# A hybrid attention and expert layer: the first sixteen row maxima read from tiles filled on the chip, one direct transfer per shift, and expert up-weights split in pieces

## The chip, the cores and the metric

One core of a Trainium2 chip runs the whole layer in one launch. The metric is the device time in microseconds of one execution; three executions were timed.

## The reference, cut to what matters

The input is 2 sequences of 1024 tokens with 128 channels. Four blocks follow, each with a residual and a layer norm: differential attention, a mixture of 64 experts (8 chosen for each token, plus a shared one), an attention over heads, and the same experts again. The change touches the start of the first block and what it shares the engines with:

```python
q, k, v = split(layernorm(x) @ w_qkv.T)          # 16 heads, 2 sub-heads of 4 channels each
s = einsum('bnhd,bmhd->bhnm', qi, ki) * scale    # 32 sub-heads, each 1024 x 1024, per sequence
p = softmax(s)                                   # the maximum over the keys is taken off
a = einsum('bhnm,bmhe->bhne', p, v)              # o = a1 - lam * a2, rms norm, w_proj
h = silu(einsum('td,edf->etf', xf, W_up))        # experts, read in high and low parts
y = einsum('etf,efd->etd', h, W_down)
```

## The kernel before, in words

Every engine has its own instruction stream, written out by hand, and they meet by semaphores. TensorE does matmuls, VectorE the row maxima, ScalarE the exponentials, GpSimd small arithmetic, SyncE nearly all transfers.

**Beginning.** The tokens are four chunks of 512 columns. For each chunk VectorE takes statistics and normalizes (`stats`, `norm`), GpSimd computes the inverse roots (`root_of`), TensorE transposes (L1239) and multiplies by the query and key weights (`queries_and_keys`, L1249), and each result is split in three bf16 parts that sum to the float32 value: ScalarE writes the high part (L814), VectorE the rest (L1024), ScalarE the middle part (L818), VectorE the low part (L1029). The values (`va`, L1255) come after all chunks.

**Stacks.** The query and key parts are laid out in DRAM, in `q_stack` and `k_stack`: 16 groups of 4 sub-heads ("strips" of 32 rows), each holding six slots of 4 rows and then rows for the shift, which `fill_shift_rows` presets. `write_parts` issues twelve transfers of 256 KB for each sequence (L479). `load_max` reads a group back into `QA` and `KA`; `load_strips` reads it into `QB` and `KB`.

**Max pass.** For each group 32 items, each a 128 x 1024 tile of scores, made by two matmuls (L1296) into two PSUM banks, of which VectorE takes the negated row maximum (`NEGMAX`, L1067). The items have two places in PSUM, banks 0-1 and 2-3. There are 512 items.

**Main loop.** A quad is two items of the max pass, four score tiles (L1333) with their exponentials (L860), and the weighted values of the quad before (L1360). There are 16 x 16 quads. The max pass leads by `LEAD` quads: quads -12 to -1 only take maxima, and the last 12 only have scores, together with side work for the experts (`SIDE`): a chain of transposes, affinities and top-k that ends in a gate tile and the `GATE` transfers. `PE` runs a quad in the order: score, item, score, weighted values, score, item, score, weighted values.

**Shifts.** After 16 items GpSimd splits their 16 columns of maxima in three bf16 parts (`shift_parts`), TensorE transposes them (L1305, at quads where `shift_at` says so, five items before the scores that need them), VectorE copies the tile out (`SHT`, L1080), SyncE writes it to `shift_d` in DRAM (L530) and reads it back into rows of `QB` in four transfers (L535). So the matmul of the scores subtracts the maximum by itself. The scores of a half group wait for it (`sh_r`). In PE's order the next item stands behind those scores.

**Expert weights.** ScalarE issues the transfers of `RAWD` (L799) and `RAWU` (four, L805), copies the high part of each (`WDH` L841, `WUH` L847), and GpSimd subtracts for the low part (L627), all before the first exponential. ScalarE also evacuates the output tiles every eight quads.

## Time and profile before

| | us |
|---|---|
| median of three executions | 1083.62 |
| lowest and highest | 1078.84, 1085.8 |
| the profiled execution, device time | 1082.55 |
| its span, first to last instruction | 1080.8 |
| VectorE busy | 958.7 (89%) |
| TensorE busy | 1001.8 (93%) |
| ScalarE busy | 890.6 (82%) |

The profile is of one execution. Its page gives the busy time of each engine, a strip of 40 slices, a chain of what ended last, and the costliest groups of instructions. The trace answers closer questions: the order of instructions in a stretch, the busy time of each engine in a stretch with the clock granted to TensorE, what an engine waited for, and how long transfers took from issue to landing. "L1067" is a line of the kernel.

### The profile page before, as it was taken

How to read it: one execution, taken by the hardware profiler on the slowest of the kernel's cores; microseconds unless marked ns; L12 is line 12 of the kernel's file. 1: busy time of each engine (PE TensorE's matmuls, PEld its weight loads, DVE VectorE, ACT ScalarE, POOL GpSimd, SP SyncE). 2: the span in 40 equal slices, each digit the busy share in tenths (PEclk: the TensorE clock that was granted, in tenths of full speed). 3: DMA queues.
4: the chain of work that ended last, by engine and by line, in shares of the span. 5: the costliest groups of instructions: out<-in, count | busy, mean ns of one | idle time of the engine just before them, and what ended most of it. 6: DMA issues, size and time to landing. Idle time of an engine off the chain costs nothing.

```text
span 1080.8 us, 21671 instructions
## 1 busy us (share of the span) xinstructions
PE 1001.8 (93%) x8016; PEld 517.0 (48%) x8016; DVE 958.7 (89%) x1187; ACT 890.6 (82%) x1466; POOL 482.7 (45%) x892
## 2 busy tenths in 40 slices
PE   6389999999999999999999999999999999999998
PEld 3012222232222222222222236888777778787876
DVE  7799999999999999999999956989876978797665
ACT  4279999999999999999999987878865787688765
POOL 3363555455445645564555657443412331333331
PEclk9569999999999999999999999999999999999999
DMA  8911110111011011101110007585766566757773
GB/s 276 306 34 51 52 51 4 51 51 32 23 52 51 17 37 52 51 3 51 52 52 3 22 3 171 151 195 146 173 179 156 137 161 174 194 153 188 197 187 91
DMA packets 80474, 108.91 MB, mean 101 GB/s; under 512 B 23537, under 2 KB 33521, under 8 KB 80369
## 3 DMA queue, kind: packets, MB, share of 16 engines
q1 hardware_dynamic: 66336, 100.98, 35.0%
q10 hardware_dynamic: 14032, 6.55, 2.4%
q8 instruction: 64, 1.05, 0.4%
q14 instruction: 42, 0.34, 0.1%
HBM read 95.57 MB, written 11.93 MB: 99 GB/s over the span
## 4 chain that ended last, share of the span: by engine, by line
DVE 51%; PE 33%; ACT 5%; DMA 4%; issue 4%; SPq 1%; POOL 0%; ACTq 0%; DVEq 0%; POOLq 0%
DVE NEGMAX L1067 46%; PE PS L1458 9%; PE PS L1460 8%; PE PS L1459 8%; PE PS L1360 3%; ACT PR L860 2%; PE PS L1333 1%; DVE HF L1108 1%; DVE HL L1116 1%; DMA shift_d<-SHT 1%; DMA GATE<-gate_d 1%; ACT PS L957 1%; ACT HH L950 1%; PE PS L1239 1%; DVE XC L1014 1%
## 5 line engine op out<-in xcount | busy, mean ns | idle before, releaser
L1067 DVE TENSOR_REDUCE NEGMAX<-PS 128x1 f32<-128x1024 f32 x512 | 584.9, 1211 | 10.2 <-PE PS L1296 9.9
L860 ACT ACTIVATE PR<-PS 128x512 f32<-128x512 f32 x1024 | 539.0, 600 | 36.7 <-PE PS L1333 24.7
L1360 PE MATMUL PS<-PR,VG 128*32 128x256 f32 (+1 forms) x3840 | 321.9, 407 | 17.3 <-ACT PR L860 2.0
L1333 PE MATMUL PS<-QB,KB 32*128 32x512 bf16 x1024 | 260.1, 387 | 3.6 <-DMA QB<-shift_d 2.1
L1296 PE MATMUL PS<-KA,QA 32*128 32x512 bf16 x1024 | 204.6, 397 | 30.7 <-DVE NEGMAX L1067 22.5
L1108 DVE TENSOR_TENSOR HF<-PS,GATE 128x1024 f32<-128x1024 f32 x128 | 156.3, 1222 | 65.0 <-ACT PS L957 55.2
L957 ACT ACTIVATE PS<-PS 128x1024 f32<-128x1024 f32 x128 | 129.2, 1009 | 75.5 <-PE PS L1460 74.4
L1333 PEld LDWEIGHTS PS<-QB,KB 32*128 32x128 bf16 x1024 | 75.2, 91 | 240.5 <-ACT PR L860 138.7
L950 ACT ACTIVATE HH<-HF 128x1024 fp32r<-128x1024 f32 (+1 forms) x136 | 139.8, 1029 | 24.2 <-DVE HF L1108 23.1
L769 POOL TENSOR_TENSOR HL<-HF,HH 128x1024 fp32r<-128x1024 f32 (+1 forms) x31 | 66.8, 2154 | 165.5 <-ACT HH L950 165.5
L1360 PEld LDWEIGHTS PS<-PR,VG 128*32 128x32 f32 x3840 | 76.4, 108 | 130.7 <-issue 65.0
L1116 DVE TENSOR_TENSOR HL<-HF,HH 128x1024 fp32r<-128x1024 f32 (+1 forms) x105 | 131.9, 1257 | 7.6 <-ACT HH L950 7.5
L1458 PE MATMUL PS<-XH,WUH 128*128 128x512 f32 x256 | 107.8, 421 | 0.0
L1458 PE MATMUL PS<-HH,WDH 128*128 128x512 f32 x256 | 102.5, 400 | 2.5 <-ACT YS L967 2.5
L1460 PE MATMUL PS<-HH,WDL 128*128 128x512 f32 x256 | 101.5, 396 | 0.0
L1459 PE MATMUL PS<-XL,WUH 128*128 128x512 f32 x256 | 101.4, 396 | 0.0
L1460 PE MATMUL PS<-XH,WUL 128*128 128x512 f32 x256 | 101.1, 395 | 0.0
L1459 PE MATMUL PS<-HL,WDH 128*128 128x512 f32 x256 | 100.8, 394 | 0.0
L675 POOL TENSOR_TENSOR ORC<-OSB,MINUS 128x16 f32<-128x16 f32 x32 | 93.2, 2911 | 3.3 <-DVE OSB L1093 0.9
L641 POOL TENSOR_TENSOR SHP<-NEGMAX,ZERO 128x16 bf16<-128x16 f32 x32 | 7.0, 218 | 167.2 <-DVE NEGMAX L1067 167.1
L1296 PEld LDWEIGHTS PS<-KA,QA 32*128 32x128 bf16 x1024 | 48.3, 91 | 58.5 <-DVE NEGMAX L1067 45.1
L1458 PEld LDWEIGHTS PS<-HH,WDH 128*128 128x128 f32 x256 | 48.4, 189 | 15.4 <-ACT YS L967 4.6
(186 smaller groups left out, 971.6 us busy)
## 6 DMA issues: line engine op xcount, KB each, us to landing
GATE<-gate_d SPq DMA_DIRECT2D x256, 256.0 KB, 4.2
QA<-q_stack SPq DMA_DIRECT2D x64, 128.0 KB, 2.6
QB<-q_stack SPq DMA_DIRECT2D x16, 256.0 KB, 3.0
KB<-k_stack SPq DMA_DIRECT2D x16, 256.0 KB, 3.0
KA<-k_stack SPq DMA_DIRECT2D x60, 64.0 KB, 2.4
q_stack<-PARTS SPq DMA_DIRECT2D x12, 256.0 KB, 4.4
k_stack<-PARTS SPq DMA_DIRECT2D x12, 256.0 KB, 4.2
RAWU<-in_L_ffn_W_up_dram ACTq DMA_DIRECT2D x4, 512.0 KB, 11.6
```

Source lines behind the costliest of these rows:

```text
L860: nc.scalar.activation(PR[:, s % PRING, r, :], PS[:, SCORE_BANK[n], :], ACT.Exp, scale=SCALE_A).then_inc(p_ready, 1)
L950: nc.scalar.activation(HH[:, k, 0:u, :], HF[:, f, 0:u, :], ACT.Copy).then_inc(hh_ok, 1)
L957: nc.scalar.activation(PS[:, z:z + 2, :], PS[:, z:z + 2, :], ACT.Silu).then_inc(silu_ok, 1)
L1067: nc.vector.tensor_reduce(NEGMAX[:, hs % 2, col:col + 1], PS[:, e:e + 2, :].rearrange("p b n -> p (b n)"), axis=AX_X, op=ALU.max, negate=T ...
L1108: nc.vector.tensor_tensor(HF[:, k, :, :], PS[:, z:z + 2, :], GATE[:, h % GSLOTS, :, :], op=ALU.mult).then_inc(hf_ok, 1)
L1116: nc.vector.tensor_tensor(HL[:, k, 0:u, :], HF[:, f, 0:u, :], HH[:, k, 0:u, :].bitcast(F32), op=ALU.subtract).then_inc(hl_ok, 1)
L1296: last = mm(PS[:, e + h, :], QA[lo:lo + STRIP, u, r // 2, nt * P:(nt + 1) * P], KA[lo:lo + STRIP, u, r // 2, :], start=True, stop=True)
L1333: mm(PS[:, SCORE_BANK[n], :], KB[strip, u, mt * P:(mt + 1) * P], QB[strip, u, half * BANK:(half + 1) * BANK], start=True, stop=True).then_ ...
L1360: last = mm(PS[STRIP * r:STRIP * (r + 1), 7, cols], VG[:, u, mt, r // 2, :], PR[:, s % PRING, r, cols], start=mt == 0, stop=mt == TB - 1 a ...
L1458: mm(dst, ah, bh, start=first, stop=False)
L1459: mm(dst, ah, bl, start=False, stop=False)
L1460: return mm(dst, al, bh, start=False, stop=last)
```

## The change

- SyncE loads two chunks of the input ahead of the weights. VectorE presets `QB` and `KB`; after the parts of the first two chunks exist, SyncE copies the rows of the first group from `PARTS` to `QB` and `KB` in twelve transfers of 16 rows of 2 KB. The first 16 items read these; items 16 to 31 of the first group read `QA` and `KA` as before, which are now loaded wholly by SyncE.
- The slots of the stacks are interleaved (row, slot), and the parts of one kind go out in one transfer, six for each sequence instead of twelve.
- The low parts of chunks 0, 2 and 3 move from VectorE to GpSimd. The orders of all engines in the beginning are rewritten; TensorE runs ten matmuls whose result is not used.
- The first 16 items have three places in PSUM (banks 0-1, 2-3, 6-7).
- `LEAD` is 11; the shift tile comes one quad later (three items before its scores) and goes to `QB` by one transfer, with no DRAM in between.
- `RAWU` is loaded in 16 transfers and split in 8 pieces through the main loop: ScalarE copies 512 columns at quads 28, 44, ... 140, GpSimd subtracts. Its addition of the projection bias to `X` moves into the loop as well.

```diff
-STACK_WRITES = 16 * 2 * (len(Q_SLOTS) + 1)
+SLOTS = STRIP // HD_A
+SHIFT_SLOT = SLOTS - 1
+STACK_WRITES = 16 * 2 * 4
+FIRST_LOADS = 16 * 2 * len(Q_SLOTS)
...
-LEAD = 12
+LEAD = 11
...
-    return (g + 3) // TB if (g + 3) % TB == 0 and 0 <= (g + 3) // TB < 2 * NG else None
+    return (g + 2) // TB if (g + 2) % TB == 0 and 0 <= (g + 2) // TB < 2 * NG else None
...
+def max_slots():
+    start = []
+    for it in range(len(ITEM)):
+        start.append((0, 2, 6)[it % 3] if it < 2 * TB else 2 * ((it + 1) % 2))
+    before = [max((m for m in range(max(0, it - 3), it) if start[m] == start[it]), default=None) for it in range(len(ITEM))]
+    return start, before
+MAX_SLOT, MAX_BEFORE = max_slots()
...
-A_ITEM = ring_order(["wT"] + [("xT", c) for c in range(NCH)] + [("va", c) for c in range(NCH)] + ["centT"])
+A_ITEM = ring_order(["wT", ("xT", 0), ("xT", 1), ("xT", 2), ("va", 0), ("va", 1), "centT", ("xT", 3), ("va", 2), ("va", 3)])
+A_LATE = A_ITEM["va", 2]
...
+def up_piece(s):
+    k = (s - 28) // QPG
+    return k if s >= 28 and (s - 28) % QPG == 0 and k < UP_PIECES else None
...
@@ sync @@
+            load_x(0)
+            load_x(1)
+            sp.dma_start(WQKV[:], w_qkv.rearrange("(j p) c -> p j c", p=P)).then_inc(ld_w, 16)
+            sp.dma_start(WPRJ[:], w_proj).then_inc(ld_w, 16)
+            load_x(2)
+            load_x(3)
+            sp.wait_ge(const_ok, 2)
...
+                    step = places[1] - places[0] if len(places) > 1 else 1
+                    rows = stack[b * GPB:(b + 1) * GPB].rearrange("g r d c n -> (g r d) c n")[:, places[0]:places[-1] + 1:step, :]
+                    sp.dma_start(rows, src.unsqueeze(1).to_broadcast([P, len(places), SEQ])).then_inc(st_w[b], 16)
...
+            def first_rows(part, j):
+                tile, slots = ((QB, Q_SLOTS), (KB, K_SLOTS))[j]
+                for c in [c for c, a in enumerate(slots) if a == part]:
+                    sp.dma_start(tile[c:P:SLOTS, 0, :], PARTS[0:R * HD_A, part, j, 0:SEQ]).then_inc(first_ld, 16)
...
             fill_shift_rows(0)
+            sp.dma_start(CENT[:], cent).then_inc(ld_b, 16)
+            for j, w in enumerate((w_q, w_k, w_v, w_o)):
+                sp.dma_start(WB[:, j, :], w).then_inc(ld_b, 16)
+            sp.wait_ge(first_set, 2)
+            for part, made in enumerate((qk_hi, qk_mid)):
+                for j in range(2):
+                    sp.wait_ge(made, 2 * NCH // BATCH - 1 + j)
+                    first_rows(part, j)
+            for j in range(2):
+                sp.wait_ge(qk_lo_pool, j + 1)
+                sp.wait_ge(qk_lo, j + 1)
+                first_rows(2, j)
+            for part in range(3):
+                write_parts(0, part)
...
-            load_max(0, 0, False)
+            load_max(0, 0)
+            fill_shift_rows(1)
+            for part, (made, n) in enumerate(((qk_hi, 2 * NCH), (qk_mid, 2 * NCH), (qk_lo_pool, 6))):
+                sp.wait_ge(made, n)
+                write_parts(1, part)
+            load_max(1, 1)
+            sp.wait_ge(const_ok, 3)
...
-                sp.dma_start(shift_d[half].rearrange("a r (t n) -> (a r t) n", n=P), SHT[:, half, :]).then_inc(sh_w, 16)
-                sp.wait_ge(sh_w, 48 * s + 16 * (half + 2))
-                for r in range(R):
-                    lo = STRIP * r + SHIFT_ROW
-                    sp.dma_start(QB[lo:lo + 3, u, half * BANK:(half + 1) * BANK], shift_d[half, :, r, :]).then_inc(sh_r, 16)
+                sp.dma_start(QB[SHIFT_SLOT:P:SLOTS, u, half * BANK:(half + 1) * BANK], SHT[:, half, :]).then_inc(sh_r, 16)
...
                     shift_rows(s, half)
+                    if s < UP_PIECES:
+                        load_up(2 * s + half)
...
@@ gpsimd @@
+            def low_part(c):
+                cols = slice(c * BANK, (c + 1) * BANK)
+                for j in range(2):
+                    n = D_ITEM["qk", j, c]
+                    pool.wait_ge(qk_mid, n + 1)
+                    nc.gpsimd.tensor_tensor(PARTS[:, 2, j, cols], R1[:, n % 4, :], PARTS[:, 1, j, cols], op=ALU.subtract).then_inc(qk_lo_pool, 1)
             for c in range(NCH):
                 root_of(("a", c))
+            for c in (0, 2, 3):
+                low_part(c)
...
+            low_weights(0, WDL[:], RAWD[:], WDH[:])
+            pool.wait_ge(ld_mix, 16 * 9)
+            for j in range(2):
+                link(nc.gpsimd.tensor_tensor(lam_p[:, j, :], LAM[:, 2 * j, :], LAM[:, 2 * j + 1, :], op=ALU.mult))
...
+            shift_parts(0)
             values(0, 0)
             values(1, 1)
-            link(nc.gpsimd.memset(ZERO[:], 0.0))
-            shift_parts(0)
-            low_weights(1, WUL, RAWU, WUH)
             for n, (dst, src, hi) in enumerate(((WSUL, RAWSU, WSUH), (WSDL, RAWSD, WSDH))):
-                low_weights(n + 2, dst, src, hi)
+                low_weights(n + 1, dst[:], src[:], hi[:])
...
+                if hs == 3:
+                    pool.wait_ge(ln_xn, NCH)
+                    nc.gpsimd.tensor_tensor(X[:], X[:], BPROJ[:].unsqueeze(1).to_broadcast([P, NT, DIM]), op=ALU.add).then_inc(xb_ok, 1)
+                if hs >= 6 and hs % 2 == 0 and hs // 2 - 3 < UP_PIECES:
+                    low_up(hs // 2 - 3)
...
@@ scalar @@
+            transposed(0)
+            high_part(0, 0)
+            transposed(1)
+            high_part(1, 0)
+            middle_part(0, 0)
+            high_part(0, 1)
+            high_part(1, 1)
+            middle_part(1, 0)
+            middle_part(0, 1)
+            middle_part(1, 1)
+            transposed(2)
+            values(0)
+            values(1)
+            centroids()
+            high_part(0, 2)
+            transposed(3)
+            high_part(1, 2)
+            middle_part(0, 2)
+            middle_part(1, 2)
+            high_part(0, 3)
+            high_part(1, 3)
+            middle_part(0, 3)
+            middle_part(1, 3)
+            values(2)
+            values(3)
             act.wait_ge(ld_down, 16)
             nc.scalar.activation(WDH[:], RAWD[:], ACT.Copy).then_inc(w_hi, 1)
-            for part in range(4):
-                load_up(part)
-            act.wait_ge(ld_exp, 32)
-            act.wait_ge(ld_up, 16 * 4)
-            for dst, src in ((WUH, RAWU), (WSUH, RAWSU), (WSDH, RAWSD)):
-                nc.scalar.activation(dst[:], src[:], ACT.Copy).then_inc(w_hi, 1)
             act.wait_ge(lam_in, 1)
             nc.scalar.activation(lam_e[:], lam_s[:], ACT.Exp).then_inc(lam_exp, 1)
+            act.wait_ge(ld_exp, 32)
+            for dst, src in ((WSUH, RAWSU), (WSDH, RAWSD)):
+                nc.scalar.activation(dst[:], src[:], ACT.Copy).then_inc(w_hi, 1)
...
+            def high_up(k):
+                cols = slice(k * BANK, (k + 1) * BANK)
+                act.wait_ge(ld_up, 16 * UP_PARTS // UP_PIECES * (k + 1))
+                nc.scalar.activation(WUH[:, cols], RAWU[:, cols], ACT.Copy).then_inc(w_hi, 1)
...
+                if up_piece(s) is not None:
+                    high_up(up_piece(s))
...
@@ vector @@
+            nc.vector.memset(QB[:, 0, :], 0.0).then_inc(first_set, 1)
+            nc.vector.memset(KB[:, 0, :], 1.0).then_inc(first_set, 1)
             for c in range(NCH):
                 dve.wait_ge(ld_x[c], 16)
                 stats(("a", c))
-                if c:
+                if 1 <= c <= 2:
                     norm(("a", c - 1))
-            norm(("a", NCH - 1))
-            for c in range(NCH):
-                rest_and_low(c)
-            dve.wait_ge(ld_mix, 16 * 9)
-            for j in range(2):
-                link(nc.vector.tensor_tensor(lam_p[:, j, :], LAM[:, 2 * j, :], LAM[:, 2 * j + 1, :], op=ALU.mult))
-            nc.vector.tensor_reduce(lam_s[:], lam_p[:], axis=AX_X, op=ALU.add).then_inc(lam_in, 1)
-            link(nc.vector.tensor_scalar(SUBW[:], SUBW[:], 1.0 - LAMBDA_INIT, None, ALU.mult))
+            rest(0, 0)
+            norm(("a", 2))
+            rest(1, 0)
+            rest(0, 1)
+            rest(1, 1)
+            low_part(0, 1)
+            low_part(1, 1)
+            norm(("a", 3))
...
+            for c in range(2, NCH):
+                rest(0, c)
+                rest(1, c)
...
@@ tensor @@
+            def warm(times):
+                for _ in range(times):
+                    mm(PS[:, 7, :], identb[:], ONES[:, 0:BANK], start=True, stop=True)
             pe.wait_ge(ident_ok, 1)
+            pe.wait_ge(identb_ok, 1)
+            pe.wait_ge(const_ok, 2)
+            warm(4)
...
+            warm(6)
+            transposed(0)
+            copied(0)
+            query_or_key(0, 0)
+            transposed(1)
+            query_or_key(1, 0)
+            copied(1)
+            query_or_key(0, 1)
+            query_or_key(1, 1)
+            transposed(2)
+            values(0)
+            values(1)
+            centroids()
+            copied(2)
+            query_or_key(0, 2)
+            query_or_key(1, 2)
+            transposed(3)
+            copied(3)
+            query_or_key(0, 3)
+            query_or_key(1, 3)
+            values(2)
+            pe.wait_ge(first_ld, FIRST_LOADS)
...
-                    e = 2 * (it % 2)
-                    if it >= 2:
-                        pe.wait_ge(m_free, it - 1)
+                    e = MAX_SLOT[it]
+                    if MAX_BEFORE[it] is not None:
+                        pe.wait_ge(m_free, MAX_BEFORE[it] + 1)
+                    elif e == 6:
+                        pe.wait_ge(qk_r1, len(D_ITEM))
...
+                    if hs == 0:
+                        strip = slice(STRIP * r, STRIP * (r + 1))
+                        for h in range(2):
+                            last = mm(PS[:, e + h, :], QB[strip, 0, nt * P:(nt + 1) * P],
+                                      KB[strip, 0, h * BANK:(h + 1) * BANK], start=True, stop=True)
+                        last.then_inc(m_full, 1)
+                        if it == 1:
+                            values(3)
+                        continue
+                    if a == 0 or hs == 1:
```

## Rows read from the trace of the kernel before

**Rows 1.** The page: the costliest group, busy time, mean of one, idle before, releaser
```profile
L1067 DVE TENSOR_REDUCE NEGMAX<-PS 128x1 f32<-128x1024 f32 x512 | 584.9, 1211 | 10.2 <-PE PS L1296 9.9
```
**Rows 2.** Stretches: length, PE, PEld, DVE, ACT, POOL busy, granted clock, DMA share, GB/s
```profile
20.00:30.00 10.00, 6.79 (x40) 4.68 (x38) 8.04 (x18) 7.91 (x17) 0.00 (x0) 1.00 0.86 319
40.00:50.00 10.00, 5.28 (x18) 0.82 (x17) 10.00 (x10) 0.00 (x0) 4.49 (x1) 0.50 1.14 359
60.00:70.00 10.00, 8.75 (x44) 1.53 (x44) 9.11 (x9) 6.70 (x14) 8.94 (x2) 0.50 0.01 2
100.00:200.00 100.00, 94.88 (x1029) 29.60 (x1025) 99.85 (x93) 94.75 (x187) 51.86 (x124) 1.00 0.15 42
625.60:654.00 28.40, 25.85 (x265) 9.56 (x258) 12.28 (x41) 24.77 (x49) 19.80 (x41) 1.00 0.04 12
```
**Rows 3.** What VectorE waited for from 80 to 610 us: total, times, longest
```profile
DVE NEGMAX L1067 <- PE PS L1296: 1.3, 5, 0.3
```
**Rows 4.** The chain of waits, first 110 us: start, length, what
```profile
26.35 2.87 DMA k_stack<-PARTS
36.30 21.57 DVE NEGMAX L1067 x19
```
**Rows 5.** Timeline of the beginning: start, length, engine, line, what
```profile
12.07 3.62 PE L1249 MATMUL PS<-XT,WT 128*128 128x512 f32 x4
12.42 1.11 DVE L1014 TENSOR_SCALAR XC<-X,ln_mv,ln_inv 128x128 f32<-128x128 f32 x4
16.34 2.23 PE L1249 MATMUL PS<-XT,WT 128*128 128x512 f32 x4
16.53 1.23 ACT L818 ACTIVATE PARTS<-SQ 128x512 bf16<-128x512 f32 x2 [0.20 <-DVE SQ L1024]
18.41 0.60 PE L1239 MATMUL PS<-ident,XC 128*128 128x128 f32 x4
26.11 1.29 DVE L1029 TENSOR_TENSOR PARTS<-SQ,PARTS 128x512 bf16<-128x512 f32 x2 [0.17 <-ACT PARTS L818]
28.11 0.38 DVE L1047 TENSOR_REDUCE T<-ident 128x8 f32<-128x128 f32 x1
28.85 0.23 DVE L1049 COPY BLK<-H 128x128 f32<-128x128 f32 x1
31.99 3.62 ACT L841 ACTIVATE WDH<-RAWD 128x4096 fp32r<-128x4096 f32 x1 [3.15 <-issue]
35.68 8.81 POOL L627 TENSOR_TENSOR WDL<-RAWD,WDH 128x4096 fp32r<-128x4096 f32 x1 [20.94 <-ACT WDH L841]
```
**Rows 6.** VectorE's low parts of the experts: duration in ns min/median/max
```profile
L1116 DVE TENSOR_TENSOR HL<-HF,HH x105: 684/1215/2977, 660.9 to 1072.4; 128x1024 fp32r<-128x1024 f32 x104, 128x512 fp32r<-128x512 f32 x1
```
**Rows 7.** Timeline of SyncE, then ScalarE's issues of RAWU, ns min/median/max
```profile
26.35 0.61 SPq L479 DMA_DIRECT2D k_stack<-PARTS  x1
59.78 1.20 SPq L535 DMA_DIRECT2D QB<-shift_d  x4
652.09 10.28 SPq L573 DMA_DIRECT2D GATE<-gate_d  x10
L805 ACTq DMA_DIRECT2D RAWU<-in_L_ffn_W_up_dram x4: 572/3502/4652, 32.0 to 40.0; - x4
```
**Rows 8.** Transfers of the first 60 us: count, KB each, median us to landing
```profile
q_stack<-PARTS SPq DMA_DIRECT2D x12, 256.0 KB, 4.4
BPROJ<-in_L_attn_a_b_proj_dram SPq DMA_DIRECT2D x1, 64.0 KB, 9.0
```
**Rows 9.** Timeline of a shift copy, and landing of the DRAM write behind each
```profile
77.68 0.21 DVE L1080 COPY SHT<-PS 48x128 bf16<-48x128 bf16 x1
DMA to landing us min/median/max: 1.3/1.4/2.9
```
**Rows 10.** The page: gate transfers, median to landing
```profile
GATE<-gate_d SPq DMA_DIRECT2D x256, 256.0 KB, 4.2
```
**Rows 11.** Timeline of VectorE: its first gated product after the attention
```profile
658.60 2.35 DVE L1108 TENSOR_TENSOR HF<-PS,GATE 128x1024 f32<-128x1024 f32 x2
```

More of the change, by code:

```diff
@@ L116, in score_tiles @@
                 tiles["out", output_at(g)] = len(tiles)
-        if shift_at(g) is not None:
-            tiles["shift", shift_at(g)] = len(tiles)
+            if p == 1 and shift_at(g) is not None:
+                tiles["shift", shift_at(g)] = len(tiles)
     return tiles
@@ L364, in hybrid_layer @@
         OTS = sb("OTS", [P, 2, BANK], where=attn)
-        SHP = sb("SHP", [P, 2, 3 * SHIFTS], BF16, where=attn)
-        SHT = sb("SHT", [3 * SHIFTS, 2, P], BF16, where=attn)
+        SHP = sb("SHP", [P, 2, R, 4, SHIFTS // R], BF16, where=attn)
+        SHT = sb("SHT", [4 * SHIFTS, 2, P], BF16, where=attn)
         ZERO = sb("ZERO", [P, SHIFTS], where=attn)
@@ L646, in shift_parts @@
                 pool.wait_ge(sh_split, (4 * hs + 3))
-                nc.gpsimd.tensor_tensor(SHP[:, u, 2 * w:3 * w], SHR[:], SHP[:, u, w:2 * w], op=ALU.subtract).then_inc(sh_split, 1)
+                nc.gpsimd.tensor_tensor(SHP[:, u, :, 2, :], rest, SHP[:, u, :, 1, :], op=ALU.subtract).then_inc(sh_split, 1)
                 pool.wait_ge(sh_split, (4 * hs + 4))
-            low_weights(0, WDL, RAWD, WDH)
-            for b in range(BATCH):
-                pool.wait_ge(st_w[b], STACK_WRITES)
+            link(nc.gpsimd.memset(ZERO[:], 0.0))
@@ L773, in _ @@
                 side(where)
-                if where == NQ - 11:
+                if where == NQ - 10:
                     heads_norm(2 * NG - 3)
@@ L1233, in ring @@
                     pe.wait_ge(free, n - 3)
-                put((0 if items is A_ITEM else 4) + n % 4).then_inc(full, 1)
+                put(a_bank(n) if items is A_ITEM else 4 + n % 4).then_inc(full, 1)
             def transposes(tiles):
@@ L1377, in quad @@
                     weighted_values(s - 1, 0)
+                if shift_at(s) is not None:
+                    shift_tile(shift_at(s))
                 if scored:
```

225 lines of the change are left out of this document (103 added, 122 removed).

## The prediction

> **What bounds the kernel now.** I read the page first. One line, the row maximum on VectorE, is busy 584.9 us of the 1080.8 us span and sits idle only 10.2 us before its instructions [rows 1]. The stretches of time say where it rules: from 100 to 200 us VectorE is busy 99.85 of 100, TensorE 94.88, ScalarE 94.75 [rows 2], and over 530 us of the loop the maxima waited 1.3 us in all [rows 3]. So the attention lasts as long as its 512 maxima, and nothing that another engine saves there counts, while 5% of slack is all that either neighbour has. The chain of waits then shows where the maxima begin: the write of the key stack and the read back precede 36.30 us, after which 19 maxima run in 21.57 us, 1.13 each [rows 4]. VectorE had finished all parts at 27.4 (26.11 + 1.29 [rows 5]), those of the first sequence earlier. The gap from 27.4 to 36.3 is the trip through DRAM. That trip is what the change takes out.
>
> **The first maximum.** With the rows copied on the chip, the limit becomes the order of work on VectorE. Its old work ended at 27.4 (26.11 + 1.29). Of its 16 rests and low parts, at 1.29 a pair, six go to GpSimd: minus 6 x 0.645 = 3.9. The three constants, 28.11 to 29.08, now stand ahead of the maxima: plus 1.0 [rows 5]. That gives 24.5. ScalarE, with 0.62 for each middle part, and TensorE, with 1.12 for a product at the full clock (2.23 for two items against 3.62 at half clock, 12.07 and 16.34 [rows 5]), come out at the same time when I lay the three orders side by side; the ten unused matmuls keep TensorE from being late, by bringing the full clock to the first chunk. One thing more: the low parts on GpSimd and on VectorE both read two tiles of SBUF at once. In the experts, where both engines do exactly that, VectorE's instruction takes 1215 ns as a rule but up to 2977 [rows 6], so one can stand behind the other. I add 0.5, for one GpSimd low part of about 1.1 (8.81 for 4096 columns [rows 5]) met half way: **25.0 us**.
>
> The Trainium skill (SBUF — State Buffer, "SBUF: two separate sides") says the pair of ports that the two share is locked for a whole instruction and the loser blocks fully. The trace's 2977 ns agrees. By that rule alone up to three meetings of 1.1 us would be possible here, so a start 3 us later.
>
> The twelve row transfers do not decide. SyncE issues four small ones in 1.20 [rows 7], so twelve in 3.6, most of them before the last low part at 18.5; landing takes 4.4 in the busy early stretch [rows 8], so they land by 23.2. The bound above: a small transfer issued into that crowd landed after 9.0 [rows 8], which gives 27.5 for the start. The bound below is 24.0, if the port meeting is nothing and the full clock comes earlier. Gain: 36.3 - 25.0 = **11.3** (8.8 to 12.3).
>
> **The third place in PSUM.** Between 40 and 50 us VectorE was busy 10.00 of 10 with two places, at half clock [rows 2]. There is nothing to win: 0. It only covers the value matmuls put behind item 1. In both versions these 16 items take 18.1 us.
>
> **SyncE until the first shift.** Now SyncE must have come past 41 issues between the last small rows (18.5) and the shift: 6 stack writes, 9 constants, 8 loads, 2 fills, 6 writes, 8 loads, 2 shared weights. At 0.65 each (0.61 and a gap [rows 7]) this is 26.7: 45.2. The shift copy comes 21.6 after the first maximum, at 46.6. So it fits, by 1.4. Data: 8.5 MB at 319 to 359 GB/s [rows 2] take 24 to 27 us from 18.5, 43 to 45.5. It fits too, barely. But the merged writes are three times as large, and four large transfers in a crowded queue took 572 to 4652 ns to issue [rows 7]. If each of the twelve costs 1.0 rather than 0.65, SyncE arrives at 49.4, and the first scores with it; behind it also ScalarE, whose first exponential now waits for the shared weights, the last two of the 41. Cost 0 to 4.5; I take **0.5**, nearer the 0.61 row, since these are pieces of 2 KB as there and the 2 MB of `RAWU` that crowded the queue from 32 us on are gone. The group for items 16 to 31 is wanted at 43 and is issued by about 34: covered by 18 us of maxima. GpSimd: `WDL` takes 8.81 after `WDH` of 3.62 [rows 5], started at about 26, done at 38.6 against 43.1, when the first shift is split.
>
> **The direct shift.** The copy lasts 0.21, the write to DRAM landed 1.4 after its issue (1.3 to 2.9) [rows 9]. For one hop in place of two I take the same: 1.65 after the copy's start. The deadline shrinks by two items of 1.13: three maxima (3.4) and the copy's 0.1, less one score and one item on TensorE, 0.7, leaves 2.8. So it is in time as a rule, and 0.3 late at the slowest. Loss **0.2** (0 to 9, if all 32 are at the slow end). Queued behind a late shift are the scores and, in TensorE's order, the next item, so lateness goes straight to VectorE.
>
> **Weights in pieces.** `WUH` and the `RAWU` transfers lay beside the maxima and cost nothing on the path. Eight copies of 512 columns, 0.62 each by a middle part [rows 5], now interrupt the exponentials: 5.0 us of ScalarE where it has 5% slack, 0.96 for eight quads. They stand three quads after the output copies, when that slack is partly used. Bounds 0 and 5.0; I take **1.0**. GpSimd is half busy [rows 2] and its bias and low pieces stay hidden; without that cover each low piece would cost 1.1.
>
> **One quad less of lead.** The total is lead-in, 512 maxima, and a tail of `LEAD` quads. The tail was 28.4 us for 12, ScalarE 24.77 of it [rows 2]: 2.06 a quad. But the gate chain begins relative to the last maximum as before: the first gate transfers, issued from 652.09 at about 0.6 each [rows 7], land 4.2 later [rows 10], at 656.9, and the first gated product ran at 658.60 [rows 11]. So only **1.7** is free (0 to 2.1); next late is the gate.
>
> **Half clock at the first scores.** TensorE ran at 0.50 from 40 to 70 us, and VectorE lost 0.89 of 10 in the last ten [rows 2]. With little to do in the lead it will be at half clock again: 0. If it stays at 1.00, a gain of 0.9.
>
> **Sum.** 11.3 + 1.7 - 0.5 - 0.2 - 1.0 = 11.3 off 1082.55, the profiled execution (span 1080.8 and 1.75 around it), which is 1.07 below the median of the three: 1071.3, and I say **1071.5**.
>
> **Rivals.** (1) *SyncE late*: twelve merged writes above 1.0 each; first scores and first exponential late by 4. For it: issue times up to 4652 ns in a crowd. Against: 0.61 for the same rows, in the full stretch before 27 us. Result 1075. (2) *ScalarE becomes the bound* at the eight pieces and pays them whole: 1075.5. For it: 94.75 busy; against: TensorE's two places ahead of VectorE absorb about 0.7 (an item of 1.13 less its two matmuls of some 0.4). (3) *The shift late every time*, the slower outcome: a half group's scores wait on a transfer onto sixteen-row-spread partitions that lands like the gate transfers, 4.2 after issue [rows 10]. From 2.8 on each microsecond is paid 32 times: (0.25 + 4.2 - 2.8) x 32 = 53, less 11.5: 1124. Against it: 16 KB, not 256, and 1.4 in the nearest row. It decides from a landing of 3.3 on, where it has eaten the gain. (4) *The start does not move as said*, because rows, ports or orders hold it to 27.5 or later: 1074. (5) *All well*: start at 24.0, full clock kept, no late wait: 1068.
>
> **Chances.** Forecast 0.47, (1) 0.19, (2) 0.10, (3) 0.04, (4) 0.08, (5) 0.12. About 1% is what a measurement of this kernel can tell from no change; that is 10.8 us, below 1072.8. The forecast gives it in four of five cases, (5) always: 0.51. Slower by over 1% only in (3): 0.04. Within: 0.45. For the range I go down to 1065 (case 5 and executions that spread by 0.4%) and up to 1080, (1) and (2) together with the late start.
>
> **What would show it.** Right: first maximum at 24 to 26 us; `SHT` about 21.6 later; no wait of the maxima above 0.3 through the loop; SyncE at the shift before VectorE's copy; the last maximum about 11 us earlier; about 1 us of waits near quads 28 + 16k. Wrong: waits of the scores on the transfer to `QB` in many periods (3), a first exponential that starts late behind shared weights (1), or a first maximum after 27.

## The result, and the profile after

The changed kernel takes 1085.96 us (median of 19 executions, 1081.33 to 1094.18), the kernel before 1081.13 (19 executions beside them, 1078.59 to 1085.8). The ratio is 1.0046, 95% interval 1.0032 to 1.0059: slower by 4.8 us. The forecast was 1071.5, within 1065 to 1080; the time lies above the range. The profiled execution after has a span of 1087.0 us, that of before 1080.8. Labels in this part: "L1157" is now the maximum, "L1430" the products of the items from `QA` and `KA`, "L1420" those from `QB` and `KB`, "L1469" the scores, "L1170" the copy of the shift tile. In the experiments the same lines have slightly other numbers. A ratio and its interval compare a kernel with the executions of the kernel before that stood beside it; it is not exactly the quotient of the two medians.

The page's line of the maximum, busy time, mean of one, idle before it and its releaser:

```profile
L1157 DVE TENSOR_REDUCE NEGMAX<-PS 128x1 f32<-128x1024 f32 x512 | 585.2, 1211 | 15.7 <-PE PS L1430 15.1
```

Against [rows 1] the work is the same, 585 us. The idle time is 15.7 instead of 10.2, and 15.1 of it waits for a product. The timeline of VectorE from 25 to 70 us shows where:

```profile
25.62 21.59 DVE L1157 TENSOR_REDUCE NEGMAX<-PS 128x1 f32<-128x1024 f32 x19
47.13 0.21 DVE L1170 COPY SHT<-PS 64x128 bf16<-64x128 bf16 x1
47.26 3.47 DVE L1157 TENSOR_REDUCE NEGMAX<-PS 128x1 f32<-128x1024 f32 x3
60.28 4.62 DVE L1157 TENSOR_REDUCE NEGMAX<-PS 128x1 f32<-128x1024 f32 x4 [9.55 <-PE PS L1430]
65.95 1.22 DVE L1157 TENSOR_REDUCE NEGMAX<-PS 128x1 f32<-128x1024 f32 x1 [1.06 <-PE PS L1430]
```

The first maximum runs at 25.62 instead of 36.30 [rows 4]: 10.7 us won. Nineteen maxima and the copy follow as before. Then three more, and VectorE stands still for 9.55 us. The product that it waits for stands in TensorE's order behind scores, and the scores wait for the shift, as the list of TensorE's waits shows (total, times, longest):

```profile
PE PS L1469 <- DMA QB<-SHT: 10.4, 1, 10.4
```

The timeline of SyncE says why the shift was late. It lists issues (start, length, destination and source); I leave out the lines inside runs of equal ones:

```profile
15.86 1.96 SPq L514 DMA_DIRECT2D QB<-PARTS  x3
22.98 0.53 SPq L514 DMA_DIRECT2D KB<-PARTS  x1
23.56 0.58 SPq L508 DMA_DIRECT2D q_stack<-PARTS  x1
...
28.60 1.64 SPq L508 DMA_DIRECT2D k_stack<-PARTS  x1
30.28 1.83 SPq L532 DMA_DIRECT2D LAM<-n_L_attn_a_lambda_q_dram  x1
...
36.20 0.49 SPq L548 DMA_DIRECT2D QA<-q_stack  x1
...
41.21 0.59 SPq L500 DMA_DIRECT2D q_stack<-ZEROS  x1
...
42.35 0.90 SPq L508 DMA_DIRECT2D q_stack<-PARTS  x1
...
48.74 1.24 SPq L508 DMA_DIRECT2D k_stack<-PARTS  x1
50.02 1.25 SPq L548 DMA_DIRECT2D QA<-q_stack  x1
...
57.16 0.47 SPq L563 DMA_DIRECT2D RAWSD<-in_L_ffn_Ws_down_dram  x1
57.73 0.59 SPq L578 DMA_DIRECT2D QB<-SHT  x1
```

The shift tile was ready at 47.3 and SyncE issued its transfer at 57.73. It was never idle in between; it worked off its list. ScalarE came no earlier, since the shared weights are the two issues before the shift. Its timeline:

```profile
59.21 0.31 ACT L924 ACTIVATE WSUH<-RAWSU 128x128 fp32r<-128x128 f32 x1 [18.20 <-DMA RAWSD<-in_L_ffn_Ws_down_dram]
60.26 2.06 ACT L941 ACTIVATE PR<-PS 128x512 f32<-128x512 f32 x4 [0.54 <-PE PS L1469]
```

Were these issues slow because of the data, or by themselves? Stretches of four microseconds tell (length, busy PE, PEld, DVE, ACT, POOL, granted clock, DMA share, GB/s):

```profile
28.00:32.00 4.00, 2.38 (x8) 0.46 (x8) 4.00 (x4) 2.81 (x1) 2.40 (x6) 0.90 1.03 377
32.00:36.00 4.00, 3.59 (x9) 0.43 (x8) 4.00 (x5) 0.00 (x0) 4.00 (x1) 0.50 0.33 103
36.00:40.00 4.00, 3.70 (x8) 0.45 (x8) 4.00 (x4) 0.00 (x0) 3.93 (x2) 0.50 0.50 124
44.00:48.00 4.00, 2.54 (x9) 0.46 (x7) 4.00 (x5) 0.00 (x0) 1.37 (x6) 0.50 1.03 376
100.00:200.00 100.00, 93.12 (x1001) 29.58 (x993) 97.21 (x90) 93.10 (x184) 57.74 (x126) 1.00 0.18 48
```

Both. During the large writes (24 to 30, 42 to 50 us) the DMA engines are full, share 1.03 and 377 GB/s, and the issues run little ahead of the data: one sequence's six writes are 3.1 MB, 8.3 us at that rate, and took 6.7 and 7.7 to issue. During the constants and the eight loads (32 to 40) they are half empty, share 0.33 and 0.50: there the issues themselves are the limit. The last row, compared with [rows 2], shows that VectorE is busy 97.21 us from 100 to 200 us, no longer 99.85; in the four stretches of 100 us behind it, it is busy 99.26 to 99.97. What VectorE waited for, first from 58 to 620 us, then from 80 to 615 (total, times, longest):

```profile
DVE NEGMAX L1157 <- PE PS L1430: 15.1, 15, 9.6
DVE NEGMAX L1157 <- PE PS L1430: 3.9, 11, 0.9
```

The second answers to 1.3 in [rows 3]. The last maximum ends at 627.99 (614.16 in before plus 11.48 is 625.64). So after a start that is 10.7 earlier, the end of the maxima is 2.35 **later**: 12.4 us more of waits (15.1 against 1.3 and 1.4 more before 80 us) and 0.6 of small pauses.

The shift's landing, from issue, min/median/max, answers to [rows 9]; the page's gate transfers to [rows 10]:

```profile
DMA to landing us min/median/max: 1.7/1.8/3.7
GATE<-gate_d SPq DMA_DIRECT2D x256, 256.0 KB, 4.1
```

And the tail, on VectorE's timeline, answers to [rows 11]:

```profile
659.56 1.22 DVE L1198 TENSOR_TENSOR HF<-PS,GATE 128x1024 f32<-128x1024 f32 x1 [0.74 <-DMA GATE<-gate_d]
661.73 1.23 DVE L1198 TENSOR_TENSOR HF<-PS,GATE 128x1024 f32<-128x1024 f32 x1 [0.94 <-DMA GATE<-gate_d]
```

SyncE issues the first gate transfer at 654.54, 26.55 us after the last maximum; before it was 652.09, 26.45 after. The products now wait for the gate. The first sum of the experts (ScalarE's first copy into `YS`) runs at 716.88 (713.67 before), 3.2 later.

### The profile page after: what moved, and what is told of

The parts are those of the page before. It is cut to its first block, busy times and chain, and to the rows that moved or that the text cites. A ratio compares the mean times of both kernels' runs of the same rounds, so it can differ in the third digit from the quotient of the medians.

```text
span 1087.0 us, 21613 instructions
## 1 busy us (share of the span) xinstructions
PE 1009.2 (93%) x8026; PEld 521.4 (48%) x8026; DVE 957.0 (88%) x1179; ACT 889.2 (82%) x1473; POOL 492.1 (45%) x911
## 4 chain that ended last, share of the span: by engine, by line
PE 37%; DVE 36%; ACT 11%; DMA 6%; issue 5%; SPq 4%; POOL 0%; DVEq 0%; ACTq 0%; POOLq 0%
DVE NEGMAX L1157 30%; PE PS L1594 7%; ACT PR L941 7%; PE PS L1496 7%; PE PS L1596 7%; PE PS L1595 7%; PE PS L1469 4%; DMA GATE<-gate_d 3%; DVE HF L1198 2%; SPq L508 1%; DVE HL L1206 1%; DMA RT<-mixed_d 1%; PE PS L1478 1%; DMA mixed_d<-VP 1%; PE PS L1329 1%
## 5 line engine op out<-in xcount | busy, mean ns | idle before, releaser
L1157 DVE TENSOR_REDUCE NEGMAX<-PS 128x1 f32<-128x1024 f32 x512 | 585.2, 1211 | 15.7 <-PE PS L1430 15.1
L1469 PE MATMUL PS<-QB,KB 32*128 32x512 bf16 x1024 | 262.8, 387 | 15.0 <-DMA QB<-SHT 10.4
L1430 PE MATMUL PS<-KA,QA 32*128 32x512 bf16 x992 | 195.0, 390 | 14.9 <-DVE NEGMAX L1157 12.1
L1469 PEld LDWEIGHTS PS<-QB,KB 32*128 32x128 bf16 x1024 | 78.4, 91 | 239.0 <-ACT PR L941 117.9
L1430 PEld LDWEIGHTS PS<-KA,QA 32*128 32x128 bf16 x992 | 46.8, 91 | 34.9 <-DVE NEGMAX L1157 25.6
```

Of the source, the lines that this page charges most:

```text
L1157: nc.vector.tensor_reduce(NEGMAX[:, hs % 2, col:col + 1], PS[:, e:e + 2, :].rearrange("p b n -> p (b n)"), axis=AX_X, op=ALU.max, negate=T ...
L1430: last = mm(PS[:, e + h, :], QA[lo:lo + STRIP, u, r // 2, nt * P:(nt + 1) * P], KA[lo:lo + STRIP, u, r // 2, :], start=True, stop=True)
L1469: mm(PS[:, SCORE_BANK[n], :], KB[strip, u, mt * P:(mt + 1) * P], QB[strip, u, half * BANK:(half + 1) * BANK], start=True, stop=True).then_ ...
```

## The experiments

The theories, by the names that the expectations use: **T1**, SyncE's list decides: the shift is late because of the issues ahead of it. **T2**, the data decide: the DMA engines had too much to move in the first 55 us, in whatever order or queue. **T3**, a quad less of lead gives nothing, since the gate chain starts relative to the last maximum. A plain count, 0.65 for each issue taken off the list, stood beside them, and later a theory on the notice of the shift.

**e1: the nine constants ahead of the first rows.** A move inside SyncE's list (the two comments stand for nine lines each):

```diff
             for j, w in enumerate((w_q, w_k, w_v, w_o)):
                 sp.dma_start(WB[:, j, :], w).then_inc(ld_b, 16)
+            # the nine transfers into LAM, BPROJ, SUBW, BO, EBIAS
             sp.wait_ge(first_set, 2)
...
-            # the same nine, after write_parts(0, part)
```

> The changed kernel with one edit: SyncE issues the nine constants (LAM, BPROJ, SUBW, BO, EBIAS) in the gap that its queue has before the first row copies, at about 10 to 15 us, instead of between the stack writes and the loads. Theory T1 (the 9.6 us stall of the maxima at the first scores is SyncE's issue order: the shift transfer was issued at 57.7 us, 10.6 after the shift copy): the 5.9 us of constants leave the queue, but the load of the first group then waits for the last stack write to land, at about 34.9 where it now starts at 36.2, so SyncE gains only about 1.3 and the stall falls from 9.6 to about 8.3. Theory T2 (the 16 DMA engines are the limit, not the issuing): the stall stays at 9.6. A plain count of issues, as in my prediction, says 9.6 - 5.9 = 3.7. First maximum stays at 25.6, at most 0.5 later. Time: 1084.5 by T1, 1086 by T2, 1080 by the plain count.

Measured: 1086.01 us (1081.41 to 1096.59, 10 executions), ratio 1.0043 [1.0016, 1.0070]. VectorE's timeline:

```profile
47.00 0.21 DVE L1170 COPY SHT<-PS 64x128 bf16<-64x128 bf16 x1
58.97 3.49 DVE L1157 TENSOR_REDUCE NEGMAX<-PS 128x1 f32<-128x1024 f32 x3 [8.38 <-PE PS L1430]
```

Taking 5.9 us of issues out moved the shift by 1.3 only (57.73 to 56.4). SyncE's timeline shows what took their place:

```profile
28.50 1.25 SPq L508 DMA_DIRECT2D k_stack<-PARTS  x1
34.88 0.49 SPq L548 DMA_DIRECT2D QA<-q_stack  x1
```

From 29.75 to 34.88 SyncE issues nothing. It waits until the six writes have landed, because the loads behind them read what they wrote. In the changed kernel the constants filled just this wait. So the plain count fails and T1 holds only with that wait in the list: the late shift is made of issues *and* of a landing. The stall fell to 8.38, where T1 said 8.3 and T2 9.6; the time, 1086.0, is the one that T2 gave, and can't tell the two apart.

**e2: the list split over two queues** (from e1). SyncE goes straight on to the second sequence's writes; ScalarE issues the sixteen loads and the shared weights.

```diff
@@ sync @@
-            sp.wait_ge(st_w[0], STACK_WRITES)
-            load_max(0, 0)
...
-            load_max(1, 1)
-            sp.wait_ge(const_ok, 3)
-            sp.dma_start(RAWSU[:, 0:F], ws_up).then_inc(ld_exp, 16)
-            sp.dma_start(RAWSD[0:F, :], ws_down).then_inc(ld_exp, 16)
@@ scalar, behind WDH @@
+            act.wait_ge(const_ok, 3)
+            act.dma_start(RAWSU[:, 0:F], ws_up).then_inc(ld_exp, 16)
+            act.dma_start(RAWSD[0:F, :], ws_down).then_inc(ld_exp, 16)
+            act.wait_ge(st_w[0], STACK_WRITES)
+            load_first(0, 0)
+            load_first(1, 1)
```

> As e1, and the eight loads for the first group, the eight for the second and the two shared expert weights are issued by ScalarE, which is idle from 31 to 59 us; SyncE goes straight from the first sequence's stack writes to the second's. The bytes and their kind stay the same. T1 (issue order): SyncE is free at about 40 us, the shift transfer is issued within 0.3 us of the shift copy at 47.1, the stall falls from 9.6 to under 1, the time falls by about 9, to 1077, and beats the kernel before by 4. T2 (DMA engines saturated): the stall stays above 5, since the same 8.5 MB have to move, and the time stays above 1082.

Measured: 1082.31 us (1077.35 to 1085.56, 10), ratio 1.0000 [0.9978, 1.0022]. VectorE's timeline:

```profile
26.39 18.19 DVE L1168 TENSOR_REDUCE NEGMAX<-PS 128x1 f32<-128x1024 f32 x16
49.61 3.49 DVE L1168 TENSOR_REDUCE NEGMAX<-PS 128x1 f32<-128x1024 f32 x3 [5.04 <-PE PS L1441]
53.02 0.21 DVE L1181 COPY SHT<-PS 64x128 bf16<-64x128 bf16 x1
```

SyncE issues the shift at 53.30, 0.3 after the copy: it is no longer late. But now the 17th item waits 5.04 us, for the loads into `QA` and `KA`. They cannot start before the first writes have landed, and they stand on ScalarE's queue beside SyncE's second writes:

```profile
36.16 0.53 ACTq L918 DMA_DIRECT2D QA<-q_stack  x1
36.73 1.30 ACTq L920 DMA_DIRECT2D KA<-k_stack  x1
...
42.52 1.55 ACTq L920 DMA_DIRECT2D KA<-k_stack  x1
```

and the stretch has no free DMA time:

```profile
36.00:40.00 4.00, 3.69 (x8) 0.38 (x6) 4.00 (x5) 0.00 (x0) 4.00 (x1) 0.50 1.03 371
40.00:44.00 4.00, 2.06 (x5) 0.25 (x4) 4.00 (x5) 0.00 (x0) 1.55 (x6) 0.50 1.04 388
```

The stall and the time are what T2 gave (above 5, above 1082). So T1 holds for the shift, and T2 for what comes next: a second queue lets the loads and the writes share the same engines, and the loads, 0.60 each in the changed kernel, take 1.3 to 1.6. The Trainium skill (Trainium Kernel Development and Optimization, "Key Constraints") says that queues issued from several engines share the 16 DMA engines, and that issuing from more than one saves issue time only. The trace agrees: 1.03 to 1.04 from 28 to 44 us, and half of the stall stays.

**e3: twelve quads of lead, five items of notice** (from e2):

```diff
-LEAD = 11
+LEAD = 12
...
-    return (g + 2) // TB if (g + 2) % TB == 0 and 0 <= (g + 2) // TB < 2 * NG else None
+    return (g + 3) // TB if (g + 3) % TB == 0 and 0 <= (g + 3) // TB < 2 * NG else None
...
-    NQ - 11: [("heads_T", 0)], ...
+    NQ - 12: [("heads_T", 0)], ...
```

> As e2, with LEAD = 12 and the shift tile five items before its scores, as in the kernel before. Theory T3 (the lead gave nothing: after the last maximum the chain to the first gate transfer took 26.5 us in both traces, and the first gated products wait for the gate): same time as e2 within 1 us, the first four gated products at the same distance from the last maximum. Rival (my prediction: a quad less of lead is worth 1.7): e3 slower than e2 by 1.7. Second rival (three items of notice for the shift are too few): e3 faster than e2, by the 2 to 3 us that the maxima lose between 70 and 628 us beside the kernel before.

Measured: 1079.32 us (1077.8 to 1083.92, 10), ratio 0.9993 [0.9973, 1.0012], the interval overlapping that of e2. From the last maximum to the first expert sum it is 89.3 us, e2 has 89.4. In these two profiles a quad more costs nothing at the end, which is T3; and the loop's waits are 1.6 instead of 2.7.

**e4: two places in PSUM** for all items:

```diff
-        start.append((0, 2, 6)[it % 3] if it < 2 * TB else 2 * ((it + 1) % 2))
+        start.append(2 * ((it + 1) % 2))
```

> The changed kernel with one edit: the first 16 maxima have two places in PSUM (as all others) instead of three. My prediction's step says the third place is worth nothing: 1086 within 1 us, VectorE without a gap in the first 16 maxima except up to 0.3 us at item 2, behind the value matmuls. Rival (the third place hides the value matmuls of 0.9 to 1.8 us behind item 1): one gap of 1 us or more there, but it is given back, since the stall at the first scores ends at a time that SyncE sets: same time, stall shorter by the gap.

Measured: 1084.81 us (1082.89 to 1094.03, 10), ratio 1.0044 [1.0017, 1.0071], as the changed kernel. This profile holds an accident that is worth more than the edit. TensorE's and then VectorE's timeline:

```profile
19.42 0.27 PE L1381 MATMUL PS<-ident,CENT 64*128 64x64 f32 x1 [2.84 <-DMA WB<-in_L_attn_b_Wo_dram]
```

```profile
29.20 22.02 DVE L1157 TENSOR_REDUCE NEGMAX<-PS 128x1 f32<-128x1024 f32 x19 [0.16 <-PE PS L1420]
59.65 4.62 DVE L1157 TENSOR_REDUCE NEGMAX<-PS 128x1 f32<-128x1024 f32 x4 [4.91 <-PE PS L1430]
```

In this execution TensorE waited 2.84 us for a weight, and the first maximum ran 3.6 us later than in the changed kernel. The stall was shorter by 4.6, and the maxima resumed at 59.65 against 60.28. SyncE issued the shift at 57.10 as against 57.73. In all three profiles the maxima resume the same time after that issue: 2.55 in the changed kernel, 2.55 here, 2.56 in e1 (56.41 and 58.97). **Where the maxima begin has no effect as long as SyncE's list ends at 57.** The first nineteen maxima took 22.02 instead of 21.59: 0.4 us, in one profile each, is the most that the third place is worth.

**e5: the whole first group from the tiles on the chip** (from e1). Items 16 to 31 read `QB` and `KB` too. So the first group's eight loads go, and the wait for the landing of the first writes moves behind the second ones, where it is over:

```diff
-            sp.wait_ge(st_w[0], STACK_WRITES)
-            load_max(0, 0)
...
+            sp.wait_ge(st_w[0], STACK_WRITES)
             load_max(1, 1)
...
-                    if hs == 0:
+                    if ga == 0:
...
```

> As e1 (constants early on SyncE), and all 32 items of the first group read QB and KB, so its eight loads into QA and KA, and SyncE's wait for the first stacks to land ahead of them, are gone. ScalarE issues nothing new. T1 (order and number of SyncE's issues set the stall): SyncE passes 8 issues and a wait of about 5 us less than in e1, reaches the shift within 1 us of its copy at 47.1, and neither the wait of e2 at item 16 (5.0 us, for loads that crawled behind 4 MB of stack writes) nor the 8.4 us wait at the first scores remains: waits of the maxima under 4 us in all, last maximum at about 618 to 619, time 1077 (5 below the kernel before). Rival T2 (the DMA engines are the limit): the shift transfer or the second group's loads crawl behind the second sequence's writes; at least 4 us of waits remain between 40 and 65 us and the time is that of e2 or worse, 1081 or more.

Measured: 1080.58 us (1074.39 to 1083.45, 10), ratio 0.9995 [0.9974, 1.0015]. SyncE's timeline has the shift nine microseconds earlier:

```profile
48.06 0.59 SPq L577 DMA_DIRECT2D QB<-SHT  x1
```

and VectorE's has no stall above 1.61:

```profile
50.94 4.71 DVE L1156 TENSOR_REDUCE NEGMAX<-PS 128x1 f32<-128x1024 f32 x4 [0.31 <-PE PS L1419]
57.25 10.49 DVE L1156 TENSOR_REDUCE NEGMAX<-PS 128x1 f32<-128x1024 f32 x9 [1.61 <-PE PS L1419]
602.31 14.88 DVE L1156 TENSOR_REDUCE NEGMAX<-PS 128x1 f32<-128x1024 f32 x13
```

The last maximum ends at 617.19, 10.8 us before that of the changed kernel: 7.9 by this edit (in e1 it ends at 625.07) and 2.9 by the constants moved in e1. The waits and the last maximum are as T1 said, or better; the time is not. T1 gave 1077, and the medians give only 5.4 of the 10.8. The executions of this kernel spread over 9 us, and the profiled one took 1076.8, 3.8 less than their median.

**e6: weights ahead of the fills** (from e5), because e4 had shown a late weight.

```diff
-            fill_shift_rows(0)
             sp.dma_start(CENT[:], cent).then_inc(ld_b, 16)
...
+            fill_shift_rows(0)
```

> As e5, and SyncE issues the loads of the centroids and the four matrices of the second attention ahead of the presets of the stacks. In the profile of e4 TensorE waited 2.84 us for the last of them in the middle of the beginning, its clock fell to 0.54 to 0.61, and the first maximum came at 29.2 instead of 25.6. Theory T4 (that load lands now early, now late, and makes the start of the changed kernel vary): first maximum at 25.5 to 26, TensorE waits nothing for WB, and the executions spread less; median 0 to 2 us under e5. Rival (the load was in time in most executions, or the presets now delay something else): same as e5.

Measured: 1079.22 us (1074.36 to 1083.97, 10), ratio 0.9988 [0.9965, 1.0010]. No effect that can be told, and the executions spread no less (9.6 us): the first maximum ran at 26.02, and its product waited 2.3 for the rows into `KB` instead.

**e7: twelve quads of lead, five items of notice** (from e6, the edit of e3).

> As e6 with LEAD = 12 and five items of notice for each shift. T3 (the tail after the last maximum is the gate chain, so a quad less of lead gives nothing): no slower than e6, and up to 1.5 us faster, since e2 against e3 showed 2.7 against 1.6 us of small waits in the loop. Rival (once the stall is gone the shorter lead shows): e7 slower than e6 by 1.7.

Measured: 1075.81 us (1073.89 to 1079.47, 9), ratio 0.9961 [0.9944, 0.9979]. This one is faster than both kernels. Its median is 3.4 below that of e6, more than the 1.5 at most that T3 gave, though the intervals overlap; that the shorter lead would show once the stall is gone (e7 slower by 1.7) is excluded. Run again on another chip as **e11**, it took 1075.71 (4 executions), ratio 0.9943 [0.9922, 0.9963].

> e7 again, word for word, beside e9 and e10 on the same chip: 1075.8 within 1.5 us, 5 below the kernel before.

**e8: without the ten unused matmuls** (from e6):

```diff
-            warm(4)
...
-            warm(6)
```

> As e6 without the ten unused matmuls. My prediction's step: they bring TensorE to its full clock before the first query and key products. If so, without them the first two or three products take 1.7 to 1.8 instead of 1.1, the high parts of the first chunks come 1 to 2 us later, and the first maximum comes 0.5 to 2 us later. Rival: TensorE would be ready earlier (the transposes of the first chunk start at 8.7 instead of 10.2) and the later cold products eat just that: first maximum within 0.3 us of e6.

Measured: 1078.02 us (1071.42 to 1083.05, 10), ratio 0.9964 [0.9936, 0.9992]. The first maximum ran at 26.75, 0.7 after e6 and 1.1 after e7. TensorE's timeline has the reason, first in e6, then in e8:

```profile
10.01 1.13 PE L1346 MATMUL PS<-XT,WT 128*128 128x512 f32 x2 [0.69 <-ACT XT L860]
```

```profile
10.25 2.07 PE L1345 MATMUL PS<-XT,WT 128*128 128x512 f32 x2 [0.69 <-ACT XT L860]
```

The first two products took 2.07 instead of 1.13, the next six 3.92 instead of 2.88. So the unused matmuls do what the prediction wanted of them. The profile's column of the granted clock reads 1.00 in both from 8 to 16 us, and also in the kernel before from 10 to 18 us, where the prediction speaks of a half clock [rows 5]: there only the durations show the difference. The times cannot tell e8 from either e6 or e7.

**e9: three items of notice** (from e7) and **e10: the high parts of the pieces on GpSimd** (from e7):

```diff
# e9
-    return (g + 3) // TB if (g + 3) % TB == 0 and 0 <= (g + 3) // TB < 2 * NG else None
+    return (g + 2) // TB if (g + 2) % TB == 0 and 0 <= (g + 2) // TB < 2 * NG else None
# e10, gpsimd, ahead of low_weights(3 + k, ...)
+                pool.wait_ge(ld_up, 16 * UP_PARTS // UP_PIECES * (k + 1))
+                nc.gpsimd.tensor_copy(WUH[:, cols], RAWU[:, cols]).then_inc(w_hi, 1)
# e10, scalar
-                if up_piece(s) is not None:
-                    high_up(up_piece(s))
```

> As e7 (LEAD = 12, first group from QB and KB, constants and weights early) with one edit: the shift tile comes three items before its scores, as in the changed kernel, instead of five. Theory T5 (three items are too few when a shift transfer lands late, 3.0 to 3.7 us instead of 1.8): typical executions as e7, some longer by 1 to 4 us, so a median 1 to 3 us above e7 and a wider spread, and waits of the maxima in the loop above e7's 1.6 us when a late landing falls in the profile. Rival (the wider spread of e5 and e6 comes from LEAD = 11, by the gate chain after the last maximum): same median and spread as e7.

> As e7, and the eight high parts of the up-weights are copied by GpSimd, just ahead of its low parts, instead of by ScalarE between exponentials. In e6 the maxima waited 0.25 us once in each 16 quads for the first eight groups. Theory (ScalarE's eight pieces cause these): the regular 0.25 us gaps vanish, waits of the maxima from 80 to 615 us fall from 1.6 to under 0.6, time 1 to 2 us lower (hard to tell apart in the times). Rival (GpSimd, delayed by one more operation of 0.5 to 1 us per piece, is late with shifts): waits appear at the shift copies instead.

Measured: e9 1077.36 us (1072.88 to 1079.93, 5), ratio 0.9935 [0.9908, 0.9963]; e10 1074.54 (1072.68 to 1079.36, 9), ratio 0.9940 [0.9924, 0.9956]; e11, on the same chip, 0.9943. The three cannot be told apart by time. The waits of VectorE from 80 to 615 us can tell them apart, in one profile each. First e7, then e9; in e10 there is none:

```profile
DVE NEGMAX L1156 <- PE PS L1429: 1.6, 8, 0.2
```

```profile
DVE NEGMAX L1156 <- PE PS L1429: 3.3, 11, 0.6
```

Eight waits of 0.2, one for each of the eight pieces, are gone when ScalarE no longer copies them. The pieces cost 1.6 in all. Three items of notice add waits of up to 0.6 and 1.7 in all. What TensorE's weight loads waited for shows whose lateness it is, first in e9 from 80 to 615 us, then in the kernel before from 80 to 610:

```profile
PEld PS L1468 <- DMA QB<-SHT: 5.8, 14, 0.4
```

```profile
PEld PS L1333 <- DMA QB<-shift_d: 6.4, 9, 1.1
```

With three items of notice the scores of 14 half groups wait for the shift, 0.4 each. With five and the direct transfer (e3, e7, e10, e11) none does.

## Why the prediction was wrong

**The step that failed is "SyncE until the first shift".** It took 0.5 us, with 4.5 as its bound; the runs show 9.55. The list has 41 issues, as counted. I had it run from 18.5 at 0.65 each to 45.2. It ran from 23.56 to 57.73: 5.1 us late at its start, 7.5 too long. Piece by piece, from SyncE's timeline:

| | forecast | measured |
|---|---|---|
| twelve row copies | 3.6, done by 18.5 | 7.7 (15.86 to 23.56) |
| twelve merged writes | 7.8 | 14.4 (6.7 + 7.7) |
| nine constants | 5.9 | 5.9 |
| sixteen loads | 10.4 | 11.5 (5.0 + 6.5) |
| four fills and shared weights | 2.6 | 2.3 |

Two sizes were wrong, one wait was not seen, and count and data were each checked alone. A row copy was priced by the four small reads of [rows 7], 1.20 for four; it took 0.62. And the merged writes were priced like one of their thirds, with the warning beside it that at 1.0 or more each SyncE would be at 49.4. They took 1.2. Six merged writes need 6.7 us where the twelve unmerged ones of the first sequence took 7.7 (19.25 to 26.96 in the kernel before), so merging saved little there: the bytes are the same. (No run has the changed kernel with unmerged writes.) The row of 0.61 was no price from an idle machine. This is the kernel before in the stretch of that row (length, busy times, granted clock, DMA share, GB/s):

```profile
26.00:28.00 2.00, 1.39 (x10) 0.96 (x9) 1.79 (x6) 2.00 (x6) 0.00 (x0) 1.00 1.03 384
```

At 384 GB/s 256 KB take 0.68 us, so 0.61 for an issue was about the price of its data, and a merged write has on average twice that data. **Where the DMA engines are full, a price goes with the bytes, and one taken from a transfer of 256 KB does not hold for one of 512 or 768.** The prediction's two sums, 26.7 by count and 24 to 27 by data, each seemed to fit. They don't run side by side: from 32 to 40 us the queue paid by count with the engines half empty, around it by data, and the whole took 34.2. The wait that was not seen is the one for the landing of the first writes, 5.1 us in e1. It cost the changed kernel nothing only because 5.9 us of constants stand in it.

Rival (1) named this mechanism, with both things that wait, the shift and the first exponential. It was given 4 us and a chance of 0.19. What it lacked was a later start of the list, since the row copies stand ahead of the 41 and took twice their price. With 9.55 instead of 4 it cancels most of the gain of 10.7; e5 takes the list's load away and the stall with it, and e4 shows that the start is of no account as long as the list is late. No run moved the shift alone to an idle queue.

**One quad less of lead: 1.7 forecast, none of it found in the changed kernel.** The step had the gate as next late, and credited the gap up to the first gated product. Counted from the end of the last maximum, that product did come earlier, at 31.6 (659.56) for 33.0 (658.60). But each product has its own gate transfer, and now each waits for it, 0.74, 0.94 and 0.81. The third runs at 36.9 after the last maximum (664.89), in before at 36.7 (662.34). The 1.4 us were gone within two products, and to the first expert sum it is 88.9 instead of 88.0. e2 and e3 show the same from the other side, 89.4 and 89.3. e6 and e7 do not quite: 87.3 with the shorter lead, 88.3 with the longer, so up to 1.0 may be there in some executions. The medians go against it in both pairs (e3 is 3.0 below e2, e7 3.4 below e6); as e3 and e7 also changed the notice, and e9, with the notice alone, can't be told from e7, what the longer lead itself brings stays open. What should have been priced is the row of gate transfers (SyncE takes 15.1 us for the first fourteen), and not only the first of them.

**The start was right**: 25.62 for 25.0, inside 24.0 to 27.5. The row copies were no limit to it: only 0.3 of TensorE's waits is put down to them (in e6 and e7 it is 2.3 and 1.4, so they are the next limit). A start 3 us later, as the rule of the port would have allowed, did not come; whether the missing 0.6 is a meeting of the two engines no run separates.

**The third place was right**: 0 forecast, 0.4 at most in e4's profile.

**The direct shift**: landing 1.8 after issue for 1.65 after the copy, and 1.7 us of waits in the loop for 0.2 (e9 against e7), by the notice and not by the hop. "In time as a rule" was too kind: in e9, as in the changed kernel, the scores wait 0.4 for it in 14 half groups. Rival (3), 53 us, is far from it: nothing lands at 4.2.

**The pieces**: 1.0 forecast, 1.6 (e7 against e10) in the profile. ScalarE as the bound (rival 2, 5.0) is excluded.

**The half clock at the first scores**: 0 forecast. The granted clock was 0.50 from 32 to 60 us, in the last eight of which TensorE did next to nothing, and still 0.50 from 60 to 68 us, as in the kernel before. The wait of 1.06 behind the stall stands for 0.89 there.

**The sum**, on the last maximum: 10.7 won at the start; 9.55 lost at the shift, 2.6 in the loop (3.9 for 1.3), 0.25 right behind the stall beyond what before had there, and 0.6 in small pauses. That is 2.35 later. The tail adds 0.9 to the first expert sum. These 3.2 us are the larger part of the 4.8 between the medians. In the experts the profile has 3 us more, 2.4 of it between the fifth and the sixth sum; in the experts the waits for `RT` are 4.5 for 1.8. This is no effect of the change: e7 and e11 are the same kernel, and that stretch takes 57.3 us in one and 53.6 in the other. Over the thirteen profiles it takes 52.6 to 57.3, and that from the third to the fourth sum 56.0 to 61.8. The remaining 1.6 of the medians stays open. Open too is why e5, whose maxima end 8.4 us earlier than in the kernel before, has a median only 0.05% below it. Its profiled execution is 5.9 shorter in span than that of before and gave 4.2 back between the fifth and the sixth sum; whether such stretches explain the medians no run shows.

## What to carry over

When a gain comes from an earlier start, list everything on the queue that carries the *next* dependent transfer, from the first issue on, and price it at the state that the queue will be in: with its data where the DMA share is near 1, with its count where it is not, and add the two, with the waits for landings that stand in the list. A small transfer on which an engine waits should not stand behind bulk work; here the remedy was a shorter list (e5: eight loads and a wait of 5 us less), since a second queue (e2) only moved the stall. And a shorter lead is worth at most what the chain behind the last unit of work leaves of it: here 1.4 us were gone within two products. Last, two profiles of one kernel (e7 and e11) differ by 3.8 us in one stretch of the experts, so read a stretch against a second profile before you explain it.

## What was not expected of the hardware

- An SBUF to SBUF copy of 16 rows of 2 KB (32 KB) took 0.53 to 0.72 us to issue, and the shift of 16 KB 0.57; up to there bytes hardly enter, 256 KB takes 0.61 [rows 7].
- What an issue costs says little of its own size: the first two writes of a sequence, 768 KB each, took 0.58 and 0.48 at 23.56, and the last two, 256 KB each, 1.38 and 1.64; the small constant behind them took 1.83, the later ones 0.43. So what an issue takes is set by what stands ahead of it, not by its own size.
- On ScalarE's queue loads of 64 to 128 KB took 1.3 to 1.6 while SyncE's writes filled the engines, 0.62 once these were done.
